# Graph sort kernel: which engine builds which lanes of the part matrix and of the value product

## What is computed

```python
x = emb[x_ids]
def _spmm(row, col, vals, x):
    return jax.ops.segment_sum(vals[:, None] * x[col], row, num_segments=N)
def _layer(x_prev, row, col, vals, W_a, b_a, W_b, b_b):
    h = _spmm(row, col, vals, x_prev)
    z = (h + x_prev) @ W_a.T + b_a + h * x_prev @ W_b.T + b_b
    return jnp.where(z >= 0, z, NEG_SLOPE * z)
# x1, x2, x3 = three layers; the output is concatenate((x, x1, x2, x3), axis=1)
```

## Time and profile before

| | |
|---|---|
| median of three runs | 9204.5 us |
| the profiled execution | 9172.53 us, its span 9170.8 us |
| pass 0, windows | 243.5 to about 1395 us |
| pass 1, windows | 1686.8 to about 2825 us |
| the three layers | about 3000 us to the end |
| busy in 1000 to 1250 us (pass 0) | ACT 249.05 of 250 us, DVE 239.72, PE 234.85, POOL 200.34 |

### The profile page before, as it was taken

How to read it: one execution, slowest core, us unless ns; L and a number is a source line. 1 busy time by engine, 2 the same in 40 slices (tenths; PEclk the granted TensorE clock), 3 DMA queues, 4 the chain that set the end, 5 groups by cost and what they waited for, 6 DMA issues and landing times.

```text
span 9170.8 us, 229058 instructions
## 1 busy us (share of the span) xinstructions
PE 8540.0 (93%) x69832; PEld 7869.9 (86%) x69833; DVE 7440.7 (81%) x11531; ACT 4551.0 (50%) x14200; POOL 5280.1 (58%) x3637
## 2 busy tenths in 40 slices
PE   7799997899995899999999999999999999999999
PEld 4577775677773799999999999999999999999999
DVE  7799996999996888877777788777777888777777
ACT  0799991699993466611112566511112566511112
POOL 8688781488783122278886122288885222388884
PEclk8899998899996899999999999999999999999999
DMA  2211110111119877788886677788887677788886
GB/s 84 38 7 7 7 7 16 11 7 7 7 7 28 189 281 280 279 283 283 285 285 241 233 279 280 276 285 285 285 285 220 252 280 281 277 283 283 285 285 202
DMA packets 1005650, 1718.93 MB, mean 187 GB/s; under 512 B 378356, under 2 KB 429624, under 8 KB 1004920
## 3 DMA queue, kind: packets, MB, share of 16 engines
q0 software_dynamic: 378656, 958.17, 34.9%
q1 hardware_dynamic: 499680, 751.43, 22.6%
q10 hardware_dynamic: 127224, 8.24, 3.2%
HBM read 961.68 MB, written 755.66 MB: 187 GB/s over the span
## 4 chain that ended last, share of the span: by engine, by line
PE 63%; DVE 2%; ACT 2%; issue 1%; DMA 1%; DVEq 0%; ACTq 0%; SPq 0%; POOL 0%; POOLq 0%
PE ps L955 35%; PE ps L946 25%; ACT work L717 2%; DVE hT L1272 1%; PE ps L963 1%; PE ps L983 1%; PE ps L984 1%; DVE work L1325 0%; PE ps L973 0%; ACTq L722 0%; DVEq L1329 0%; DVE work L1210 0%; DMA work<-messages,work 0%; DMA tile_base<-start_base 0%; DMA work<-tile_base 0%
## 5 line engine op out<-in xcount | busy, mean ns | idle before, releaser
L955 PE MATMUL ps<-work 128*128 128x125 f32 x28416 | 3294.0, 278 | 44.3 <-DVE work L1325 40.8
L955 PEld LDWEIGHTS ps<-work 128*128 128x128 f32 x28416 | 3240.0, 192 | 98.3 <-DVE work L1325 65.9
L551 POOL DMA_INDIRECT work<-messages,work x1776 | 2712.7, 1527 | 636.4 <-issue 631.7
L946 PE MATMUL ps<-xb,work 125*128 x21504 | 2450.5, 276 | 96.3 <-ACT work L717 75.9
L946 PEld LDWEIGHTS ps<-xb,work 125*128 125x128 f32 x21504 | 2419.3, 192 | 127.4 <-issue 127.4
L1325 DVE TENSOR_TENSOR work<-work,iota_p 128x1000 f32<-128x1000 f32 x1776 | 2119.5, 1193 | 35.3 <-ACT work L735 35.3
L717 ACT ACTIVATE work<-ps,work 128x128 f32<-128x128 f32 x5376 | 1532.8, 368 | 1113.5 <-PE ps L946 1113.5
L536 POOL PARTITION_BROADCAST work<-work x672 | 556.1, 829 | 2324.9 <-DMA work<-slot_cols 1260.7
L735 ACT ACTIVATE work<-work 128x8 f32<-128x8 f32 x1776 | 534.4, 301 | 2687.2 <-DMA work<-messages,work 2685.5
L843 PEld LDWEIGHTS ps<-hT 128*128 128x128 f32 x12768 | 1485.0, 196 | 302.2 <-ACT stage L648 182.7
L843 PE MATMUL ps<-hT 128*128 128x96 f32 x12768 | 1521.3, 280 | 191.2 <-ACT stage L648 188.0
(11 more groups left out here) (206 smaller groups left out, 4054.5 us busy)
## 6 DMA issues: line engine op xcount, KB each, us to landing
messages<-work SPq DMA_DIRECT2D x2688, 256.0 KB, 2.4
work<-messages,work POOLq DMA_INDIRECT x1776
out_x<-xb SPq DMA_DIRECT2D x150, 125.0 KB
sorted_edges<-stage,run_idx POOLq DMA_INDIRECT x798
work<-slot_cols SPq DMA_DIRECT2D x672, 2.0 KB
work<-lane_places SPq DMA_DIRECT2D x532, 5.2 KB
out_x<-xb ACTq DMA_DIRECT2D x4, 1562.5 KB
sorted_edges<-hT SPq DMA_DIRECT2D x4, 908.0 KB
```

Of the source, the lines that this page charges most:

```text
L551: pool.indirect_dma_start(out=ck[:, n, :, :].rearrange("p h x -> p (h x)"), out_offset=None, in_=flat, in_offset=bass.IndirectOffsetOnAxis ...
L946: last = t.matmul(ps[:, n % PR, j * D:(j + 1) * D], col_hot[:, n % OHR, j * P:(j + 1) * P], x_flat[:, bass.ds(offs[n], D)], start=True, st ...
L955: last = t.matmul(part[n], ck[:, n, j // CH, j % CH * D:(j % CH + 1) * D], sel[:, n % SELB, j, :], start=j == 0, stop=j == CHB - 1)
```

## The change

Two constants, nothing else. ScalarE makes lanes 0 to 17 of `to_part` where it made 0 to 19, and VectorE lanes 18 to 23 where it made 20 to 23. GpSimd makes lanes 0 to 17 of the value product where it made 0 to 13, and VectorE 18 to 23 where it made 14 to 23. All other operations and all waits stay as they are.

```diff
 assert P * SLOTS + 3 * P < BIG
-ACTL = 20
-POOLL = 14
+ACTL = 18
+POOLL = 18
 HW = 475
```

## The result

The changed kernel takes 9232.6 us (median; 9229.4 to 9235.2) against 9197.5 (9194.0 to 9210.0) for the kernel before: a ratio of 1.0036, 95% interval 1.0026 to 1.0046. It is slower by 35 us. The profiled execution took the same 9232.6; its span is 9230.9 us.

A forecast was written before the change was run, and what follows sets the result against it. ScalarE, 8.44 us a window, was taken to bound the sort, with VectorE next. Pass 0 (-8 + 19), pass 1 (-3 + 35) and start-up (+3) gave +46 us: 9218 profiled, 9250 median, range 9168 to 9285.

The forecast's parts named there:

- The mechanism: Sort windows: a late GpSimd's longer product holds VectorE's `one_hot`, costing VectorE 0.52 to 0.54 us in each window.
- The bound: Sort windows: ScalarE bounds at 8.44 us; after the change it needs 7.66 and VectorE, at 8.10 to 8.15, bounds.
- late state: GpSimd's scatters and product run late, the product overlapping `one_hot`: windows of 8.64 us in pass 0, 8.69 in pass 1.
- the 0.78 us: ScalarE's saving per window from two lanes fewer: 0.58 us on the `Abs` steps and 0.2 on the `Relu`.
- The product: GpSimd's value product with four lanes more: proportional price 1.95 ns a column, +0.374 us, to 1.68 us.
- if 0.2 us of it were fixed: Alternative price of GpSimd's longer product: with 0.2 us fixed, four lanes add 0.32 us.
- How the state is entered: A 3.0 us landing puts the third scatter in L1142, then a first scatter in `one_hot`; 23 windows on time, then 10.
- That nothing ends it: Late windows last: at 8.64 us VectorE leaves TensorE 0.7 us, and a slow `order`, 1.6 us longer, stays hidden.
- The sum: Both sort passes against the profiled 9172.5 us: -8 + 19, -3 + 35 and +3 for start-up, together +46 us.
- Half and half: Rival: something ends the late windows again and again; 9198 us with half late, 9174 with a third; mixed chance 0.18.
- Late from the start: Rival: all windows of both passes late, +64 us, 9268; no separate chance given.
- Always on time: Rival: GpSimd catches up after long landings, or they come only in profiled executions; -76 us, 9128; chance 0.18.

The follow-up runs named there:

- experiment 7: Changed kernel with two scatters instead of three per window of pass 1: 9152.1 us, ratio 0.9963 to before; the changed kernel rerun beside it: 9214.0 us, 1.0034.
- experiment 6: (18, 16) plus six 128-column GpSimd products into an unused tile, once, ahead of pass 1's loop: 9184.9 us, ratio 1.0003 to before.
- (18, 17): Changed kernel with 17 lanes of the value product on GpSimd instead of 18: 9205.5 us, ratio 1.0019 to before.
- (18, 16): Changed kernel with 16 product lanes on GpSimd instead of 18: 9132.4 us, ratio 0.9952 to before; on a second chip 9133.5 us, 0.9947.
- the pushes: experiment 6, and the same one-time products added to the changed kernel with 14 GpSimd lanes: 9191.3 us, ratio 1.0005 to before.
- (18, 15): Changed kernel with 15 product lanes on GpSimd instead of 18: 9150.1 us, ratio 0.9964 to before.

## Why the prediction was right, and where its sizes were off

I forecast 9250 in 9168 to 9285, and slower; it is 9233 and slower. The mechanism is the one forecast. That the excess over before came so near, +35 us for +46, is in part luck: the passes gave 27 of it (below).

**The bound.** Right. ScalarE's window, row by row, in the late state: two rows of its timeline in the kernel after,

```profile
1002.24 5.37 ACT L659 ACTIVATE hT<-iota_p,place 128x128 f32<-128x128 f32 x18 [0.89 <-DVE place L1135]
1007.64 2.13 ACT L662 ACTIVATE hT<-hT 128x2304 f32<-128x2304 f32 x1
```

5.37 for 5.94 and 2.13 for 2.34, and 0.89 us idle: the 0.78 us were there. L1142 took 0.952 us (0.684 + 0.267 forecast), L1116 0.458, and windows on time 8.10 in pass 0, 8.10 and 8.20 in turn in pass 1: as worked out.

**The product.** Mis-sized: 1.63 us, not 1.68. The proportional price was wrong; 1.31, 1.47 and 1.63 us for 672, 768 and 864 columns make 1.67 ns a column and some 0.19 us fixed, which is what the "if 0.2 us of it were fixed" of my text gives. The Trainium skill's 2.6 cycles an element, from the GPSIMD Engine Reference, section 3.1, would have been further off: by an estimate from it 0.42 us for four lanes, against 0.32 measured. A late window therefore costs 0.50 us and not 0.54: over some 206 late windows 8 us of the forecast's excess.

**How the state is entered.** Right in kind and nearly in place: 3.12 us for the first landing where I had 3.0, the third scatter held inside L1142, a first scatter in `one_hot`. In pass 0 it came after 21 windows (I had 23). In pass 1 it came after 32, not 10: the first long landing, 2.92 us, did no harm, and the windows stayed on time until the next, at 1897. That is 22 windows at 0.5, 11 us. Between the long landing and the fall lie windows in which the third scatter is held and no first scatter falls into `one_hot` yet: 2 in pass 0 and 8 in pass 1, and 14 in pass 0 of the second profile of this kernel (experiment 7). I had five; that number is chance, and so is part of the forecast's nearness.

**That nothing ends it.** Right: the late state lasted to the end of both passes in this profile, through windows of 9.04 to 9.31 us behind slow `order`s and long landings; a slow `order` had ended it before. Most slow `order`s, 7.22 us for 5.59, were hidden as forecast. Some took 8.8, longer than I had allowed for; behind the one at 805 us L1142 waited 0.26 us, as this row of after shows, and the state held all the same.

```profile
813.90 0.96 DVE L1142 TENSOR_TENSOR hT<-place,iota_p 128x768 f32<-128x768 f32 x1 [0.26 <-PE ps L843]
```

The push of experiment 6 and the removal of a scatter in 7 show the same from both sides.

**The sum.** Profile against profile I had +46 us for the two passes; they gave 11 + 16 = 27. With 8 + 11 us for the two misses above it is the 46. The other 33 us of the 60 between the profiles were in no term. 20 are behind the last window of pass 1, where nothing changed. There the profile of after is the odd one: it takes 6377 us, before takes 6357, and the eleven profiles of the experiments 6352 to 6365, with 6360 for the same kernel in experiment 7. The kernel before was slower beside the result as well, with a median of 9197.5 against 9180.6 to 9188.2 beside the experiments. So most of the 20 probably belongs to where the result was measured and not to the change; no trace shows it. 13 are ahead of the first steady window, where VectorE's L1148 waits for the first value product behind GpSimd's row gathers: the rows of after and before,

```profile
275.66 1.36 DVE L1148 TENSOR_TENSOR hT<-place,iota_s 128x1152 f32<-128x1152 f32 x1 [17.05 <-POOL hT L494]
```

```profile
260.79 1.36 DVE L1148 TENSOR_TENSOR hT<-place,iota_s 128x1152 f32<-128x1152 f32 x1 [3.38 <-POOL hT L494]
```

All experiments, whatever their sizes, had a longer form of it, with waits of 12.3 to 17.1 us, and before has only one profile here. Whether the change lengthens the start-up or that one execution was lucky stays open. The median of before lies 25 us above its profiled execution and that of after 0; so the medians' +35 contains the +27 of the passes and 8 us that I can't place. In experiment 7 the same kernel is 29 us over before on one chip, and its passes take 23 us more than in the profile of before.

**The rivals.** Half and half is what the profiles of (18, 17) and, on the second chip, (18, 16) show. Late from the start was what the pushes made. Always on time is what the profile of (18, 15) shows, 38 us under before.

## What to carry over

Two edits that are free or good alone (0 and -25 us) can cost 29 to 35 together, when one takes away the slack that hid the other's coupling; so work out what a helper engine does to the engine that has just become the bound, not only whether it fits in the window. With such a feedback the share of late windows is the cost, and it shows as a spread between executions (50 us with 17 lanes, where before spread over 24). The best size run was neither kernel's: (18, 16) is 0.5% under before, with both profiled executions late in the last part of pass 0 (for 3 and for 63 windows), and (18, 15) gives 0.36% with no late window in its one profile.

## What the runs showed of the hardware

- A `tensor_tensor` on GpSimd holds a VectorE `tensor_scalar` of 128x24 with one fp32 input in SBUF for as long as it runs: 1.16 us for 0.18. I had thought that only operations with two inputs are held. `one_hot` is held until about 0.12 us before the product's end.
- An indirect scatter doesn't hold VectorE in return. In the window on time above a scatter runs from 470.11 to 471.68 and the two-input operations beside it keep their length, as these rows of VectorE in the kernel after show. Here the trace differs from the exclusive lock of the Trainium skill (SBUF — State Buffer, "SBUF: two separate sides"), where the one that starts first blocks the other; only the scatter, when it comes second, is held. (For two-input operations the section lets the lock count only against a GpSimd instruction that reads SBUF; that the scatter is held suggests it is one.)

```profile
470.39 0.46 DVE L1116 TENSOR_TENSOR hT<-hT,work 128x288 f32<-128x288 f32 x1
470.76 1.35 DVE L1118 TENSOR_TENSOR hT<-hT,work 128x1152 f32<-128x1152 f32 x1
```

- Two queues that are each below the bound kept each other late for over a hundred windows after a single push of 3.6 us.
